# Moving one triangular inverse of an attention kernel from GpSimd to VectorE, with the order of the work around it

## The reference

```python
x = x + 0.5 * moe(layernorm(x), gate_w, wi_gate, wi_up, wo)   # top 2 of 8 experts
x = x + attn(layernorm(x), ...)
x = x + 0.5 * moe(layernorm(x), gate_w, wi_gate, wi_up, wo)
```

```python
q = l2norm(q); k = l2norm(k); v = v * beta; kb = k * beta
attn = -(kb @ k.T) * strict_lower                  # 32 x 32 for each chunk and head
for i in range(1, chunk):                          # the inverse, row after row
    attn[i, :i] += attn[i, :] @ attn[:, :i]
attn = attn + eye
u = attn @ v; w = attn @ kb
for each chunk:                                    # the scan
    u_c = u_c - w_c @ S
    o_c = q_c @ S + (q_c @ k_c.T * incl_lower) @ u_c
    S = S + k_c.T @ u_c
```

## Time and profile before

| what | value |
|---|---|
| time, median of 3 runs | 1117.05 us (1116.97 to 1122.63) |
| time of the profiled execution | 1120.73 us |
| span of the profiled execution | 1118.9 us |
| busy in the span: PE, DVE, ACT, POOL | 854.6, 543.9, 335.9, 465.5 us |
| mean granted TensorE clock | 0.898 of full |
| matmuls | 11563 |

### The profile page before, as it was taken

The page is one execution under the profiler, slowest core; times in us unless marked ns, Lnnn a source line. Parts: engine busy times, 40 slices in busy tenths (PEclk is TensorE's granted clock), DMA queues, the critical chain, the costliest instruction groups (busy, mean ns, idle before and its releaser), DMA issues. The chain is left out here.

```text
span 1118.9 us, 26929 instructions
## 1 busy us (share of the span) xinstructions
PE 854.6 (76%) x11563; PEld 751.8 (67%) x11563; DVE 543.9 (49%) x1569; ACT 335.9 (30%) x646; POOL 465.5 (42%) x588
## 2 busy tenths in 40 slices
PE   4419999969558579988998899797526999799800
PEld 3419999969546457776777678665415999799800
DVE  6715565625455024575566356622623555445333
ACT  2214444324122112342234325311413444334200
POOL 1664479842233820870185028302024420323076
PEclk9999999979868869999999999986656999989955
DMA  7333434523100000000000000000004434334113
GB/s 266 131 109 112 142 116 125 157 88 94 56 26 2 0 22 4 2 20 32 4 2 21 4 4 1 21 4 21 1 17 139 133 125 136 107 118 143 55 40 110
DMA packets 68467, 75.71 MB, mean 68 GB/s; under 512 B 8150, under 2 KB 55165, under 8 KB 67836
## 3 DMA queue, kind: packets, MB, share of 16 engines
q1 hardware_dynamic: 60156, 57.27, 16.2%
q0 software_dynamic: 8192, 16.73, 4.7%
HBM read 47.82 MB, written 26.22 MB: 66 GB/s over the span
## 5 line engine op out<-in xcount | busy, mean ns | idle before, releaser
L237 POOL DMA_INDIRECT queue<-xn,slot x128 | 128.2, 1002 | 247.8 <-DVE slot L1459 104.7
L638 DVE TENSOR_TENSOR e_hid<-e_sg,e_pu 128x320 f32<-128x320 f32 x256 | 123.9, 486 | 195.8 <-ACT e_sg L594 134.1
L594 ACT ACTIVATE e_sg<-e_pg 128x320 f32<-128x320 f32 x256 | 111.6, 438 | 233.1 <-PE e_pg L556 162.4
L554 PE MATMUL e_pg<-e_xlo,e_whi 128*128 128x320 f32 x256 | 97.7, 382 | 23.6 <-issue 15.3
L243 POOL DMA_INDIRECT xn<-rows,slot x64 | 61.6, 963 | 123.2 <-ACT e_xhi L580 61.1
L684 POOL TENSOR_TENSOR a_prod<-a_inv,a_nmat 128x31 f32<-128x31 f32 (+15 forms) x124 | 64.5, 521 | 95.4 <-DVE a_nmat L1317 86.0
L541 PE MATMUL e_po<-expert,e_hid 128*128 128x128 f32 x640 | 86.2, 278 | 0.3 <-issue 0.3
L541 PE MATMUL e_po<-e_expert,e_hid 128*128 128x128 f32 x640 | 84.0, 276 | 1.3 <-DVE e_hid L638 1.3
L895 PE MATMUL a_pz<-a_vhi,lag_hi 128*128 128x512 f32 x184 | 79.3, 431 | 5.0 <-DVE a_vlo L1272 5.0
L541 PEld LDWEIGHTS e_po<-expert,e_hid 128*128 128x128 f32 x640 | 82.2, 194 | 0.5 <-issue 0.5
L541 PEld LDWEIGHTS e_po<-e_expert,e_hid 128*128 128x128 f32 x640 | 80.3, 193 | 1.8 <-DVE e_hid L638 1.8
(11 more groups left out here) (285 smaller groups left out, 1840.2 us busy)
## 6 DMA issues: line engine op xcount, KB each, us to landing
e_xs<-queue SPq DMA_DIRECT2D x32, 320.0 KB
rows<-e_rows SPq DMA_DIRECT2D x32, 320.0 KB, 2.7
expert<-wexp_in SPq DMA_DIRECT2D x14, 512.0 KB
e_expert<-wexp_in SPq DMA_DIRECT2D x14, 512.0 KB
queue<-r_zero SPq DMA_DIRECT2D x4, 1280.0 KB
expert<-wexp_in SPq DMA_DIRECT2D x14, 256.0 KB, 2.7
e_expert<-wexp_in SPq DMA_DIRECT2D x14, 256.0 KB
queue<-xn,slot POOLq DMA_INDIRECT x128
```

The lines of the kernel that those rows point to most:

```text
L237: pool.indirect_dma_start(io.queue[c], bass.IndirectOffsetOnAxis(ap=k.slot[:, j, c:c + 1], axis=0), k.xn[:, j, :], None, bounds_check=SLOT ...
L554: pe.matmul(out, whi[par][:, i, fs], xlo[par][:, cols], start=True, stop=False)
L594: act.activation(sg[n % 2][:], pg[n % 2][:, 0:HALF], ACT.Silu).then_inc(silued, 1)
L638: dve.tensor_tensor(hid[q % 2][:, f, c * HALF:c * HALF + HALF], sg[n % 2][:], pu[n % 2][:, 0:HALF], ALU.mult).then_inc(hidden, 1)
```

## The change

- In stage -1 (`ahead and not here`), VectorE calls `substitute` for group 0 (`invert_first`), in two pieces: columns 0 to 11, and, behind `cross_values`, columns 12 to 30. GpSimd still sets `inv` to the identity, increments the new semaphore `identified`, and goes on to `fetch(2)`. Groups 1 to 3 stay on GpSimd.
- `low_values` now comes behind `factors` by the code, which is where it stood before too, and ahead of the inverse.
- `normalise` of the next rows is cut in two halves of four rows, behind `mask(0)` and behind `mask(1)`.
- On ScalarE `measure` moves behind the values (`silu_values(a, 1)`). The ScalarE table for roots is then the last one loaded in the stage, so that the load ahead of `measure` goes behind the values, and stage 0 loads the other table (1 load more) ahead of its keys.

The instructions of TensorE stay as they are. VectorE gets 62 more, GpSimd 62 fewer.

```diff
             def invert(a):
-                steps = Steps(pool, subchain, a * 64)
+                steps = Steps(pool, subchain, 2 + (a - 1) * 64 if a else 0)
...
+                if not a:
+                    pool.sem_inc(identified, 1)
+                    return
                 pool.wait_ge(factored, a + 1)
                 substitute(pool, steps.done, nmat, inv, prod, 0, CHUNK - 1)
...
-            def normalise(a, mv, std, rstd, rooted, normed):
+            def normalise(a, mv, std, rstd, rooted, normed, first=0, end=GRP):
                 dve.wait_ge(rooted, a + 1)
-                link(dve.reciprocal(rstd[:], std[:]))
-                for j in range(GRP):
+                if not first:
+                    link(dve.reciprocal(rstd[:], std[:]))
+                for j in range(first, end):
...
+            def invert_first(first, last):
+                dve.wait_ge(identified, 1)
+                dve.wait_ge(factored, 1)
+                substitute(dve, link, nmat, inv, prod, first, last)
+                if last == CHUNK - 1:
+                    dve.sem_inc(inverted, 1)
...
                     mask(a, 0)
+                    if not here:
+                        normalise(g + 2, mv, std, rstd, rooted, normed, 0, GRP // 2)
...
-                if ahead and not here and n == 5:
-                    low_values(a, 0)
-                    low_values(a, 1)
...
                     mask(a, 1)
+                    if not here:
+                        normalise(g + 2, mv, std, rstd, rooted, normed, GRP // 2, GRP)
...
                     factors(a)
+                if ahead and not here and n == 4:
+                    low_values(a, 0)
+                    low_values(a, 1)
+                    invert_first(0, 12)
+                    cross_values(a)
+                    invert_first(12, CHUNK - 1)
...
-                if later and n == 5:
+                if later and here and n == 5:
                     normalise(g + 2, mv, std, rstd, rooted, normed)
...
-                if ahead:
+                if ahead and here:
                     cross_values(a)
...
-                if ahead:
+                if ahead and here:
                     measure(a)
...
                 if ahead:
                     silu_values(a, 1)
+                if ahead and not here:
+                    measure(a)
```

More of the change, by code:

```diff
@@ L764, in attention @@
         ksquared, ksummed, krooted = (sem(n) for n in ("ksquared", "ksummed", "krooted"))
-        factored, inverted = sem("factored"), sem("inverted")
+        identified, factored, inverted = sem("identified"), sem("factored"), sem("inverted")
         vlow, vhigh = sem("vlow"), sem("vhigh")
@@ L1253, in statistics @@
                 last.then_inc(varied, 1)
-            def normalise(a, mv, std, rstd, rooted, normed):
+            def normalise(a, mv, std, rstd, rooted, normed, first=0, end=GRP):
                 dve.wait_ge(rooted, a + 1)
-                link(dve.reciprocal(rstd[:], std[:]))
-                for j in range(GRP):
+                if not first:
+                    link(dve.reciprocal(rstd[:], std[:]))
+                for j in range(first, end):
                     last = dve.tensor_scalar(k.xn[:, a * GRP + j, :], tile(a, j), mv[:, j, 0:1], rstd[:, j:j + 1],
                                              ALU.subtract, ALU.mult)
-                last.then_inc(normed, 1)
+                if end == GRP:
+                    last.then_inc(normed, 1)
             def low_rows(a, b):
```

## The result

The changed kernel took 1112.64 us, the median of 8 runs (1109.31 to 1117.45); the kernel before took 1119.21 us in 8 runs between them (1116.97 to 1122.69). The ratio is 0.9941, with a 95% interval of 0.9914 to 0.9967: 6.6 us less where 19.1 were forecast, 14.6 above the predicted time and 4.6 above the upper end of the range.

The account below looks back on a forecast made before the run. Bound taken: in stage -1 TensorE waits for GpSimd's inverse, then for issue in two solves beside gathers. Inverse -10.7, solves -6.9, clock -1.5 sum to -19.1 us: 1101.6 us profiled, 1098 us as median; range 1094 to 1108.

Parts of the forecast that it names:

- The inverse on VectorE: Stage -1: 62 linked operations on VectorE take 23.6 us; with the steps around them, first solve 10.7 us earlier.
- Low values, reciprocal and `prepare`: VectorE's other steps ahead of TensorE's first solve in stage -1: 1.4, 0.3 and 1.96 us.
- rival 3: VectorE's steps in stage -1 cost about twice as much: inverse 51 us, kernel 1125 us; chance 0.04.
- The solves: TensorE's two solves, 256 matmuls, take 5.3 us instead of 12.25 once the gathers leave them: -6.9 us.
- The hidden edits: Reordered `low_values`, `measure`, table load and `normalise` halves in stage -1: covered by waits, halves fitting within 0.1 us.
- The clock: TensorE's full clock returns at 386.6 to 387.8, about when group 1's keys begin: -1.5 us, bounds 0 and -2.3.
- The gathers: Group 2's eight gathers issue behind the identity, 338.2 to about 349.1, and leave the solves: -6.9 us.
- rival 1: Waits for issue move with the gathers to the grams, 3 to 8 us late: 1101 to 1106 us; chance 0.22.
- masks that come late: Sign in stage -1: masks after 340 coming late, not at their old times, would show the waits moved with the gathers.
- The gain goes through to the end: From the scan's first update in stage 0 onward, the whole gain of 19.1 us lasts to the kernel's end.

Follow-up runs that it names:

- the gathers early: Changed kernel with group 2's gathers directly behind group 1's, ahead of the identity: 1102.12 us on chip 4, 1101.91 us on chip 14.
- the second experiment: Changed kernel, but GpSimd waits for the end of VectorE's inverse before issuing group 2's gathers, so they lie beside the solves: 1109.48 us, ratio 0.9876.

## Why the prediction was wrong

**The inverse on VectorE: right.** 23.4 us measured, 23.6 predicted. Low values, reciprocal and `prepare` cost 1.16, 0.3 and 1.9 us from start to start (1.4, 0.3, 1.96). The doubling of rival 3 did not occur: with GpSimd computing nothing, a step took 0.19 us at 31 elements, and the steps began 0.38 us apart in the mean, as forecast.

**The solves: right.** 4.94 us measured, 5.3 predicted, and the waits went with the gathers, as inferred: the kernel before with only its gathers moved gained 6.4 us of the 6.9.

**The hidden edits: right.** The order edits alone cost 0.9 us by the medians, less than the runs can tell from nothing, and 0.1 in the stretch. The halves took 1.1 us each, and the added table load lies ahead of ScalarE's next keys, which still waited 5.3 us, as the timeline of ACT shows:

```profile
393.35 1.28 ACT L1634 ACT_TABLE_LOAD   x1
399.95 0.60 ACT L1634 ACTIVATE a_kq<-a_pz 128x512 f32<-128x512 f32 x1 [5.32 <-PE a_pz L843]
```

**The clock: nearly.** The 12 keys took 4.2 us instead of 5.1, 0.9 of the 1.5 us. The clock came back only at 398.3, not by the predicted 388. Most of that is the late first solve (390.74), but not all: the prediction allowed 4.7 to 5.9 us from the first solve to full clock, and it took 7.6 here and 6.9 to 7.7 in the three kernels of chips 4 and 14 with the gathers behind the factors or early. The prediction had read its 4.7 us from the beginning of the keys, with 12.25 us of solves ahead of them, and counted it from the first solve.

**The gathers: this step failed.** The prediction saw that gathers coincide with the waits, moved them from the solves to the grams, and gave the solves their 6.9 us back. It left the grams "at their old times" and gave the case that the loss moves along only 0.22 (rival 1), priced at 3 to 8 us. It came true, and dearer, so that the time lies above the range and above rival 1's own 1101 to 1106. The sign that it had named for rival 1, masks that come late, is in the trace (348.71). The first gram took 9.65 us instead of 1.1, 8.6 more; the eight large matmuls behind it took 1.5 us more and the second gram 0.8 more, at half clock; so `factors` was 10.96 us late. The argument against rival 1, that large matmuls stand between the grams, was beside the point: one gram of 64 small ones in a row suffices, and the other three were spared because the gathers were over. The upper price was short because it took the loss of the solves (8.2 us) as its end, and left out the clock, which fell to half in the trickle and made the large matmuls behind it slower (0.79 us instead of 0.39 to 0.50 for one of L843).

The sum closes. In the stretch from the 1501st to the 2501st matmul the change took off 8.1, 8.7 and 10.7 us (each against 132.7 to 132.9; on chip 14 the order edits alone stand for the kernel before), and without the starved gram 18.8 to 19.5 us, where the terms predicted 19.1. By whole runs on one chip it is 19.0 us with the gathers early and 8.9 with them where the change puts them; with the gathers put aside, the forecast gain of 19.1 would have been about right (10.8 to 26.0 us by the ratio). The 6.6 us of the first comparison are less than the 8.1 of the stretch by 1.5, which is within the interval (3.7 to 9.6 us by the ratio).

**The gain goes through to the end: not contradicted.** In the two profiled executions of the first comparison the changed kernel is 10.1 us ahead at the first update and only 3.6 at the end; 4.0 of the 6.5 us between are in matmuls 8501 to 10001 (79.6 us against 75.6). In the pair of traces of chip 6 it is the other way: 8.7 us ahead by the stretch, 12.6 at the end, with 73.5 against 76.4 us there. So I take it for the variation of that part, and not for a cost of the change.

**Left open.** Why two chips, 1 and 15, do not starve. The difference is not one of the grams alone. In the experts, 16 gathers (L243, 214.13 to 234.23) run beside matmuls of 320 columns; the trace of before has one long wait there, the first row below, which ends as the last gather is issued, the second:

```profile
233.46 0.63 PE L554 MATMUL e_pg<-e_xlo,e_whi 128*128 128x320 f32 x1 [7.33 <-issue]
```

```profile
233.29 0.94 POOL L243 DMA_INDIRECT xn<-rows,slot  x1 [0.30 <-issue]
```

Other traces of starving chips have it too (8.6 us in the result's), two on chip 14 do not, and those of chips 1 and 15 have none. The kernel before has no trace on these chips, so whether its solves trickle there is not known; by whole runs the change gained 14.9 us on chip 1 (11.7 to 18.8 by the ratio), which hardly tells 12.2 without the solves' term from 19.1 with it. That plain traffic on SyncE's queue is harmless is shown, by one trace; that GpSimd's plain loads are harmless rests on one gram. What in a gather holds TensorE up is open (below). Of the four places tried, two are equally good: behind the factors and early, 1103.5 and 1102.1 us on one chip, both faster than before and than the changed kernel, which was timed against the second on chip 14.

## What to carry to other kernels

When waits coincide with transfers and the transfers move, ask what will be beside them at their new place, and price that before the gain is booked: here a term of 6.9 us was taken and paid back with 11.0, 8.6 of them in one gram. On chips like 4, 6 and 14, keep indirect gathers away from a burst of small matmuls that others wait for; where the queue has room, issue them earlier. Beside the large matmuls of the multiscale convolution they cost nothing here, but the wait of 7.3 us in the experts says that large matmuls are no safe place as such. Split the time at a matmul of fixed number on either side of the change: 1000 matmuls of it told 8 us apart to within 1 us, where whole runs spread by 8.

## What the hardware showed that I had not expected

- The trickle has a beat. The rows of the starved gram begin 1.44, 1.46, 0.73, 0.71, 2.14 and 0.73 us apart, each with 1 to 4 matmuls, and those of the solve in the second experiment 0.71 us and 1.44 us apart: multiples of 0.72 us. The gathers are 1.25 us apart, so it isn't their beat.
- It is no block of instructions that comes late. Instructions have a DMA queue of their own (q8). The one packet beside the starved gram was carried at 340.5 in 0.93 us, 19.3% of 16 engines in 0.3 us, as the DMA view of 340.4 to 340.7 us shows:

```profile
q8 instruction: 1, 0.02, 19.3%
```

  On chip 1 the packet in the same place took as long (19.4%). The first wait (339.88 to 341.02) was over before that packet was through (341.4). From 341.5 to 350 us, where all the other waits end, the trace has packets of the gathers' queue alone. The Trainium skill (Runtime: NRT & Kernel Launch, Instruction fetch mechanics) says that instructions come in blocks of 16 KiB, mostly hidden. The trace agrees on the size (0.02 MB in one packet); the rule does not explain the trickle.
- The starvation belongs to the chip or its state: 9.7 us for the gram on the first and on chip 6, 6.8 us on chip 14, 1.1 on chips 1 and 15. The two that do not starve are those on which the kernel before took 1069 to 1074 us instead of 1119 to 1123.
- It is the time since the gathers began that sets where TensorE stops, more than the place in the program. In all four starved grams exactly 43 matmuls went through first, but in all four the gram also began 2.1 us behind the first gather, and the stop came 3.0 to 3.1 us behind it. The solves tell the two apart: in the trace of before they began 1.3 us behind the first gather, and 123 matmuls went through, to 3.2 us; in the experiment with the gathers behind the inverse they began 2.0 us behind it, the same instructions first stopped after 46, at 2.8 us, and trickled from the 92nd on, at 3.9 us.
- One wait does stay at one place. In every trace whose solves have no gathers beside them, on starving chips and others, TensorE waits 1.1 to 1.8 us for issue behind the 152nd of the 256 matmuls (104 are left, as in the row at 394.13).
